# A fused layer (state-space scan plus experts) on one core: step 0's dt made in the first stage, x*D written straight into y's accumulator by ScalarE, softplus ahead of group 3's exponentials

## The chip, the core and the metric

The kernel runs on one core of a Trainium2 chip. The metric is the device time of one execution in microseconds (us), lower is better. The engines are named as in the profile: PE (TensorE: matmuls; PEld its weight loads), DVE (VectorE), ACT (ScalarE), POOL (GpSimd) and SP (SyncE, which here only issues DMAs). Each runs its own program in order, and they meet at semaphores. Everything is float32.

## What is computed

The input x has 2048 tokens of 512 features. The layer returns x + mamba(layernorm(x)) + experts(layernorm(x)):

```python
proj = hidden @ in_proj_w.T;  x, gate = split(proj)       # 1024 channels each
xt = silu(causal_conv4(x) + conv_b)
ts, B, C = split(xt @ x_proj_w.T)                         # 32, 16, 16 columns
dt = softplus(ts @ dt_proj_w.T + dt_proj_b)
state = state * exp(dt * A) + dt * B * x                  # per channel and 16 states, over time
y = (sum over states of state * C) + xt * D
out = (y * silu(gate)) @ out_proj_w.T
...
y = combine(silu(g) * u @ w_down)                         # 64 routed experts, top 6, 64 slots each
shared = silu(h @ sw_gate) * (h @ sw_up) @ sw_down
```

## The kernel before

There are three stages; a barrier of all engines stands between the first and the rest.

**Stage 1** (`stage1`) runs over four chunks of 512 tokens. It normalizes x, projects it (each matmul as three products of high and low parts; ACT makes the high part of a weight tile, `w_hi`, and POOL the low part, `w_lo`), convolves on DVE (`conv`), makes the router's scores and lists on DVE (`ranks`, `search`), and makes ts, B and C. SP stores what stage 2 needs and, in the last chunk, loads stage 2's first operands: the gate and up weights of the first expert pair, the tile of C (`load_C`), `load_dt` (ts and the weights of dt) and `load_xa` (xt). In the last chunk POOL also makes the first eight B diagonals.

**Stage 2** is 32 steps, one for 128 channels and 512 tokens; every step also does one pair of experts. Step i is written as i = 8c + d. A step has eight groups g of two states. In every group

- ACT copies the last column of a state buffer (`state_carry`) and makes two tiles `dA` = exp(dt * A) from `dt_blocks`, which holds dt spread over partitions;
- PE makes dt * B * x in PSUM (`dBx(i, cp, g)`, 64 short matmuls, tile p_dBx, two buffers). It first waits until the scan of group g-2 is done, which read the same buffer;
- DVE scans two states of 512 time steps (line 959), reading dA and p_dBx;
- POOL multiplies the states by C (line 894); PE adds these products over the states into the PSUM tile p_y (`sum_states(i, m, steps_ago)`, m = 0 for groups 0 to 3, m = 1 for groups 4 to 7; the latter runs in the next step, between dBx 2 and dBx 3).

The order on each engine is written out by hand. In PE's step it is dBx 0, `tokens_T`, `dt_proj(i+1)`, dBx 1, gate matmuls, dBx 2, sum_states of the last step's m = 1, `transpose_h`, dBx 3, half of the up matmuls, dBx 4, the other half, `dtx_T(i+1)`, dBx 5, `skip`, dBx 6, sum_states m = 0, dBx 7, `down`. `skip(i)` opens the accumulation of p_y: four identity matmuls that put x*D there, from a tile xD that ACT made at group 0 (`x_times_D`, line 1063) after waiting for the last step's m = 0 sum. DVE multiplies the finished p_y by the gate after the scan of group 3 (`gate`).

The dt of step i+1 is made within step i: `dt_proj`, softplus on ACT (`softplus_parts`, `softplus_log`: Abs, Relu, Exp, Ln, behind group 3's exponentials), `next_dt` and `next_dtx` on DVE behind the scan of group 1 (they make dt and dt*x in PSUM and SBUF), `take_dt` on ACT, then `spread_dt` on SP: 16 DMAs of 64 KB from SBUF to SBUF into `dt_blocks`, and `dtx_T`/`take_dtxT` for the transposed dt*x. For step 0 the same chain runs at the start of stage 2, before its first dBx. POOL meanwhile clears expert_y, expert_h, score_of_slot, silu's row and both buffers of the products, stores zeros in the spare rows of the experts' sums (DRAM tensor moe), and then gathers the first pair's tokens. ACT enters the loop after all buffers are cleared (s_c0) and those stores have landed (s_sc).

**Stage 3** computes the shared expert and the output projection and is not touched, but for the split of one buffer into two.

## Time and profile before

| | |
|---|---|
| median of 3 runs | 1401.55 us (1401.48 to 1403.74) |
| profiled execution, its own time | 1394.07 us |
| its span, first to last instruction | 1391.9 us |
| stage 1 ends, about | 267.7 us |
| stage 2 | 267.7 to 1089 us |
| busy: PE, DVE, ACT, POOL | 1307.6, 1093.6, 900.7, 882.9 us |
| mean granted TensorE clock | 0.983 |

Times in the rows are microseconds from the start of the span. A row of the timeline gives start, duration, engine, line, operation, output<-inputs, count, and in brackets the idle time before it and what ended it. Durations of neighbours overlap by some hundredths, so the step from one start to the next is the cost in a full queue.

### The profile page before, as it was taken

Reading aid. Unit: us, or ns where it says so; the run is one execution under the profiler, and the core shown is the slowest. Engines: PE = TensorE matmul, PEld = TensorE weight load, DVE = VectorE, ACT = ScalarE, POOL = GpSimd, SP = SyncE. Lnnn points to the kernel's source line nnn. Section 1 sums busy time; section 2 is a strip of 40 time slices with the busy share of each in tenths; the row PEclk is TensorE's granted clock in tenths of the full one; section 3 lists DMA queues with packets and bytes.
Section 4 is the critical chain, followed back from the end, with each engine's and each line's share of the span. In section 5 each row is a group of like instructions: output and inputs, shape, how many; then the busy total and the mean of one; then the engine's idle time right before and its main releaser. Section 6 shows DMA issues by size and latency. Waiting matters only on the chain.

```text
span 1391.9 us, 53931 instructions
## 1 busy us (share of the span) xinstructions
PE 1307.6 (94%) x21847; PEld 806.3 (58%) x21847; DVE 1093.6 (79%) x1259; ACT 900.7 (65%) x1912; POOL 882.9 (63%) x523
## 2 busy tenths in 40 slices
PE   4998989589999999999999999999999899999998
PEld 3767767345455545555545555445545577787876
DVE  4798989768988988889888898888888655655554
ACT  2756556378888778787887878867778343434343
POOL 2455357368898888988978889889898521303030
PEclk9999999789999999999999999999999999999999
DMA  7153535579899899898998989989889761313140
GB/s 287 65 223 117 197 131 204 176 195 307 264 290 286 248 289 278 274 302 238 307 268 256 298 260 292 294 248 293 271 250 298 251 230 50 132 37 144 35 146 31
DMA packets 129743, 304.84 MB, mean 219 GB/s; under 512 B 18512, under 2 KB 20304, under 8 KB 127888
## 3 DMA queue, kind: packets, MB, share of 16 engines
q1 hardware_dynamic: 122048, 285.13, 62.8%
q0 software_dynamic: 7632, 18.91, 6.0%
q8 instruction: 34, 0.56, 0.2%
q14 instruction: 29, 0.24, 0.1%
HBM read 213.65 MB, written 56.77 MB: 194 GB/s over the span
## 4 chain that ended last, share of the span: by engine, by line
PE 71%; DVE 4%; issue 3%; ACT 1%; DMA 1%; ACTq 0%; SPq 0%; DVEq 0%
PE p_dBx L1273 20%; PE p_y L1289 8%; PE p_dBx L1339 7%; PE p_g L1259 6%; PE p_u L1242 6%; PE p_g L1242 6%; PE p_dt L1222 3%; PE p_y L1350 2%; PE p_g L1350 2%; PE p_u L1350 2%; PE p_dt L1350 2%; PE p_y L1283 2%; PE p_u L1228 1%; DVE out_operand_parts L994 1%; PE p_dt L1235 1%
## 5 line engine op out<-in xcount | busy, mean ns | idle before, releaser
L959 DVE TENSOR_TENSOR_SCAN state<-dA,state_carry,p_dBx 128x512 f32<-128x512 f32 x512 | 626.7, 1266 | 87.2 <-PE p_dBx L1273 77.2
L894 POOL TENSOR_TENSOR h_times_C<-state,C_bcast 128x1024 f32<-128x1024 f32 x128 | 304.2, 2377 | 86.0 <-DVE state L959 85.2
L1106 ACT ACTIVATE dA<-dt_blocks,A_par 128x512 f32<-128x512 f32 x512 | 338.7, 709 | 18.9 <-DMA dt_blocks<-step_rows 18.8
L1273 PEld LDWEIGHTS p_dBx<-B_diagonals,step_rows 64*32 64x32 f32 x16384 | 236.1, 106 | 174.7 <-issue 174.6
L894 POOL TENSOR_TENSOR C_bcast<-state,C_bcast 128x1024 f32<-128x1024 f32 x128 | 320.0, 2787 | 17.6 <-DVE state L959 17.6
L1273 PE MATMUL p_dBx<-B_diagonals,step_rows 64*32 64x128 f32 x16384 | 314.0, 275 | 15.5 <-issue 14.5
L261 POOL TENSOR_TENSOR w_in_parts_lo<-C_bcast,w_in_parts_hi 128x512 fp32r<-128x512 f32 x64 | 89.8, 1405 | 123.1 <-ACT w_in_parts_hi L454 122.8
L909 POOL TENSOR_TENSOR step_rows<-step_rows 128x512 f32<-128x512 f32 x16 | 21.7, 1389 | 182.3 <-DMA step_rows<-moe 182.3
L1339 PE MATMUL p_dBx<-x_parts,shared_w_parts 128*128 128x512 f32 x528 | 127.3, 402 | 4.6 <-DVE shared_w_parts L988 4.6
L1339 PEld LDWEIGHTS p_dBx<-x_parts,shared_w_parts 128*128 128x128 f32 x528 | 100.6, 191 | 31.5 <-issue 7.4
L333 DVE SCALAR_TENSOR_TENSOR conv_out<-conv_in,conv_w,conv_out 128x512 f32<-128x512 f32 x96 | 94.7, 996 | 11.2 <-ACT conv_out L468 8.9
L1259 PE MATMUL p_g<-w_down_pair,step_rows 128*64 128x512 f32 (+1 forms) x396 | 92.3, 601 | 0.0
L1242 PE MATMUL p_u<-w_up_pair,step_rows 128*64 128x352 f32 x512 | 90.4, 472 | 1.3 <-issue 0.9
L454 ACT ACTIVATE w_in_parts_hi<-C_bcast 128x512 fp32r<-128x512 f32 x64 | 40.2, 630 | 73.6 <-PE p_in L577 65.9
L577 PE MATMUL p_in<-xT_parts_hi,w_in_parts_lo 128*128 128x512 f32 x256 | 72.9, 407 | 12.4 <-issue 6.1
L1242 PE MATMUL p_g<-w_gate_pair,step_rows 128*64 128x352 f32 x512 | 83.9, 470 | 0.3 <-ACT step_rows L1121 0.3
L1161 ACT ACTIVATE shared_h_rows<-p_dBx 128x512 f32<-128x512 f32 (+1 forms) x24 | 14.3, 597 | 104.9 <-PE p_dBx L1339 104.3
L874 POOL DMA_INDIRECT moe<-expert_y,scatter_rows x34 | 55.3, 1627 | 23.8 <-ACT expert_y L1079 18.6
L577 PE MATMUL p_in<-xT_parts_lo,w_in_parts_hi 128*128 128x512 f32 x256 | 69.5, 394 | 0.0
L577 PE MATMUL p_in<-xT_parts_hi,w_in_parts_hi 128*128 128x512 f32 x256 | 69.2, 392 | 0.0
L1010 DVE TENSOR_TENSOR shared_h_rows<-shared_h_rows,p_dBx 128x512 f32<-128x512 f32 (+1 forms) x24 | 16.5, 687 | 62.9 <-ACT shared_h_rows L1161 62.7
L1289 PE MATMUL p_y<-C_bcast,sum_over_states 128*32 128x512 f32 x528 | 63.5, 598 | 0.0
(172 smaller groups left out, 2018.4 us busy)
## 6 DMA issues: line engine op xcount, KB each, us to landing
w_gate_pair<-in_w_gate SPq DMA_DIRECT2D x32, 1408.0 KB
w_up_pair<-in_w_up SPq DMA_DIRECT2D x32, 1408.0 KB
w_down_pair<-in_w_down SPq DMA_DIRECT2D x66, 512.0 KB
dt_blocks<-step_rows SPq DMA_DIRECT2D x512, 64.0 KB
w_down_pair<-in_w_down SPq DMA_DIRECT2D x33, 384.0 KB
g_d<-y_gated SPq DMA_DIRECT2D x33, 256.0 KB, 4.8
sz_d<-silu_gate SPq DMA_DIRECT2D x32, 256.0 KB, 2.1
moe<-zeros SPq DMA_DIRECT2D x32, 256.0 KB, 3.0
```

What stands on the lines that cost most here:

```text
L261: pool.tensor_tensor(wp[1][:, n % 2, :], win[:, tile, :], wp[0][:, n % 2, :], ALU.subtract).then_inc(s_wlo, 1)
L333: ins = dve.scalar_tensor_tensor(xt[:, d, :], xr[:, d, k:k + CH], cw[:, d, k:k + 1], xt[:, d, :], ALU.mult, ALU.add)
L577: ins = pe.matmul(pIn[n % 2][:, :], wp[p][:, n % 2, k * P:(k + 1) * P], xp[q][:, c % 2, k, :], start=at == 0, stop=at == len(parts) - 1)
L894: pool.tensor_tensor(hc[m][:, b, :, :], hb[:, q, :, :], Cb[:, NM * cp + GS * m:NM * cp + GS * m + GS, :], ALU.mult).then_inc(s_hc, 1)
L959: ins = dve.tensor_tensor_scan(hb[:, g % NBUF, s, :], dA[:, g % NBUF, s, :], pB[:, g % 2, :].rearrange("p (t s) -> p s t", s=GS)[:, s, :], ...
L1106: ins = act.activation(dA[:, q, s, :], dtr[:, u, b, :], ACT.Exp, scale=A[:, bass.ds(d, 1), GS * g + s:GS * g + s + 1].rearrange("p a b -> ...
L1242: ins = pe.matmul(pX[r, 0:I], xgT[:, k, r], w[:, a, k, :], start=k == 0, stop=k == KH - 1)
L1259: ins = pe.matmul(pG[r, :], hT[0:k, m, r], wd[0:k, a, m, :], start=m == 0, stop=m == len(IK) - 1)
L1273: ins = pe.matmul(out[DB * p:DB * p + DB, half, j, :, :], dtxT[k, j * P + DB * b:j * P + DB * b + DB], diag[k, ND * cp + 2 * j + p // 2, a ...
L1289: ins = pe.matmul(pY[DB * b:DB * b + DB, :], sel4[:, :], hc[m][:, b, s, :], start=False, stop=m == 1 and s == GS - 1, skip_group_check=True)
L1339: ins = pe.matmul(pX[m % 2][:, :], wparts[:, m % 2, 2 * w + a, k, :], xp[x][:, k, :], start=at == 0, stop=at == len(parts) - 1)
L1350: ins = pe.matmul(pO[j][:, :], k_parts(p, k, 0)[:, j * P:(j + 1) * P], k_parts(q, k, 1), start=k == 0 and at == 0, stop=k == NK - 1 and at ...
```

## The change

1. **Step 0's dt in stage 1.** PE makes it at the end of the third chunk (into p_xT), ACT does Abs, Relu, Exp, Ln behind it (`first_softplus`), POOL the sum and dt*x in the fourth chunk behind its second `w_lo` (`first_dt`), SP the 16 spreading DMAs behind the load of the first gate weights. The tiles live in the unused end of the up weights' buffer; `dt_blocks` is split in an even and an odd tile, of which the even one doubles as stage 1's xn_T. Stage 2 starts with `dtx_T(0)`; its semaphores of step 0 are counted up.
2. **Start of stage 2.** POOL gathers first and clears three small buffers after it; the clears of the product buffers and of expert_y are gone. The zeros of moe's spare rows are copied from DRAM to DRAM at POOL's end of stage 1.
3. **x*D.** ACT writes it into p_y itself, at group 7 behind that group's exponentials; `skip` is gone, and PE waits for ACT ahead of the sum m = 0.
4. **Softplus** stands in front of group 3's carry copy and exponentials.

The core of the diff:

```diff
@@ SP, stage 1, last chunk
                     tile_in.load_gate(sp, 0)
+                    sp.wait_ge(s_dt0, 1)
+                    tile_in.load_dt(sp, 1)
+                    sp.wait_ge(s_xTs, 16 * NCH)
+                    sp.wait_ge(s_lps, NCH)
+                    sp.wait_ge(s_xlo, NCH)
+                    for b in range(NB):
+                        for p in range(NB):
+                            sp.dma_start(dtr0[DB * p:DB * p + DB, b, :], zl0[DB * b:DB * b + DB, :]).then_inc(s_spread, 16)
@@ POOL, stage 1
+            def first_dt():
+                pool.wait_ge(s_z0, 4)
+                pool.tensor_tensor(zl0, r0, zl0, ALU.add).then_inc(s_dt0, 1)
+                pool.wait_ge(tile_in.s_xa, 32)
+                pool.wait_ge(s_dt0, 1)
+                by_row = "p (i j r) -> p i j r"
+                pool.tensor_tensor(dtx[:, :].rearrange("p (j i r) -> p i j r", i=2, j=JD), zl0.rearrange(by_row, i=2, j=JD),
+                                   tile_in.xa[:, 0, :].rearrange(by_row, i=2, j=JD), ALU.mult).then_inc(s_dt0, 1)
...
+                    if c == NCH - 1 and n == 1:
+                        first_dt()
...
+            for a in range(2):
+                pool.dma_start(io["moe"][a * ROWS + T:(a + 1) * ROWS, :], io["moe"][a * ROWS:a * ROWS + CAP, :]).then_inc(keep["s_sc"], 16)
+                pool.wait_ge(keep["s_sc"], 16 * a + 16)
@@ ACT, stage 1
+            def first_softplus():
+                act.wait_ge(s_dt0ps, 1)
+                act.wait_ge(keep["s_par"], 48)
+                b = keep["dt_b"][:, 0:1]
+                act.activation(zl0, pT[:, 1, :], ACT.Abs, bias=b).then_inc(s_z0, 1)
+                act.activation(r0, pT[:, 1, :], ACT.Relu, bias=b).then_inc(s_z0, 1)
+                act.wait_ge(s_z0, 2)
+                act.activation(zl0, zl0, ACT.Exp, scale=-1.0).then_inc(s_z0, 1)
+                act.wait_ge(s_z0, 3)
+                act.activation(zl0, zl0, ACT.Ln, bias=1.0).then_inc(s_z0, 1)
@@ PE, stage 1, behind the x projection
+                if c == NCH - 2:
+                    pe.wait_ge(tile_in.s_wdt, 32)
+                    pe.wait_ge(s_xhi, NCH)
+                    pe.matmul(pT[:, 1, :], tile_in.wdt[:, :], tile_in.ts[:, :], start=True, stop=True).then_inc(s_dt0ps, 1)
@@ POOL, stage 2
-            pool.memset(yo[:, :, :], 0.0).then_inc(s_yz, 1)
-            for t in (hh[:, :], wsc[:, :], sz, hc[0], hc[1]):
-                pool.memset(t, 0.0).then_inc(s_c0, 1)
...
             gather(0, 0)
+            for t in (hh[:, :], wsc[:, :], sz):
+                pool.memset(t, 0.0).then_inc(s_c0, 1)
@@ ACT, stage 2
+            def x_times_D(i, u, d):
+                act.wait_ge(s_xa, 16 * i + 16)
+                act.wait_ge(s_g, i + 1)
+                act.activation(pY[:, :], xa[:, u, :], ACT.Copy, scale=d).then_inc(s_xD, 1)
...
-            act.wait_ge(s_sc, 32)
...
+                            if g == SOFTPLUS_AT:
+                                softplus_parts(i + 1, d + 1)
+                                softplus_log(i + 1)
                             act.wait_ge(s_scan, NG * i + (g + 1))
...
-                            if g == 0:
-                                act.wait_ge(s_sum, 2 * i + 1)
-                                act.wait_ge(s_xa, 16 * i + 16)
-                                x_times_D(u, Dp[:, bass.ds(d, 1)])
...
                             if g == NG - 1:
+                                x_times_D(i, u, Dp[:, bass.ds(d, 1)])
                                 take_dtxT(i + 1, 0, NG * i + 7)
@@ PE, stage 2
                     dBx(i, cp, 5)
-                    skip(i)
                     dBx(i, cp, 6)
+                    pe.wait_ge(s_xD, i + 1)
                     sum_states(i, 0, 0)
```

The end of a step on PE, before (line 1273 is dBx, 1283 the skip, 1289 sum_states, 1259 down):

```order
L1235 MATMUL p_dt<-identity,step_rows 128x128 x4
L1264 REGISTER_ALU
L1273 MATMUL p_dBx<-B_diagonals,step_rows 32x2x64 x32
L1283 MATMUL p_y<-step_rows,identity 32x512 x4
L1264 REGISTER_ALU
L1273 MATMUL p_dBx<-B_diagonals,step_rows 32x2x64 x32
L1289 MATMUL p_y<-h_times_C,sum_over_states 32x512 x8
```

and now (1313 is dBx, 1322 sum_states):

```order
L1275 MATMUL p_dt<-identity,dt_x 128x128 x4
L1304 REGISTER_ALU
L1313 MATMUL p_dBx<-B_diagonals,step_rows 32x2x64 x32
L1304 REGISTER_ALU
L1313 MATMUL p_dBx<-B_diagonals,step_rows 32x2x64 x32
L1322 MATMUL p_y<-h_times_C,sum_over_states 32x512 x8
```

Only the four matmuls between dBx 5 and dBx 6 are gone; everything else in the step keeps its place.

ACT between the third and the fourth chunk of stage 1, now (584 copies ts, B and C out; 529 to 534 are `first_softplus`; 541 and the rows behind it belong to the fourth chunk):

```order
L584 ACTIVATE x_proj_out<-p_logits_ssm 128x256
L529 ACTIVATE w_up_pair<-p_xT,dt_bias 128x512
L530 ACTIVATE w_up_pair<-p_xT,dt_bias 128x512
L532 ACT_TABLE_LOAD
L532 ACTIVATE w_up_pair<-w_up_pair 128x512
L534 ACT_TABLE_LOAD
L534 ACTIVATE w_up_pair<-w_up_pair 128x512
L541 ACTIVATE conv_in<-conv_in 128x8x3
L485 ACTIVATE w_in_parts_hi<-C_bcast 128x512
L498 ACTIVATE conv_in<-p_in 128x512
```

Before, the copy out and the fourth chunk's first row stood next to each other; four activations and two table loads are new between them, and a third load stands in front of the fourth chunk's first Silu.

POOL at the start of stage 2, before (844 to 847 clear and set, 850 stores the zeros, 854 and 860 gather step 0's tokens):

```order
L844 MEMSET expert_y 128x1024
L846 MEMSET expert_h 128x352
L846 MEMSET score_of_slot 128x34
L846 MEMSET step_rows 128x512
L846 MEMSET h_times_C 128x4096
L846 MEMSET C_bcast 128x4096
L847 IOTA scatter_rows 128x2
L850 DMA moe<-expert_y 64x512 x2
L854 COPY gather_rows<-gather_lists 128x1
L860 DMA tokens_of_pair<-xn_d,gather_rows 128x576
```

and now:

```order
L894 COPY gather_rows<-gather_lists 128x1
L900 DMA tokens_of_pair<-xn_d,gather_rows 128x576
L920 MEMSET expert_h 128x352
L920 MEMSET score_of_slot 128x34
L920 MEMSET step_rows 128x512
L921 IOTA scatter_rows 128x2
```

The gather moved from behind everything to the front; three of the clears and the stores are gone from here.

## Rows read from the trace of the kernel before

**Rows 1.** Windows: stage 1's last stretch, and the steps of stage 2.
```profile
196.00:267.00 71.00, 59.68 (x322) 43.43 (x320) 68.18 (x109) 33.63 (x60) 34.25 (x25) 0.96 0.58 208
361.70:1089.00 727.30, 711.95 (x17651) 367.72 (x17649) 638.84 (x611) 573.98 (x1323) 631.18 (x348) 1.00 0.91 277
```
In these rows stand: from:to, length, busy us (and count) of PE, PEld, DVE, ACT, POOL, granted clock, DMA share, GB/s.

**Rows 2.** Timeline of PE, one step of stage 2.
```profile
386.64 1.16 PE L1273 MATMUL p_dBx<-B_diagonals,step_rows 64*32 64x128 f32 x64
...
394.37 0.70 PE L1273 MATMUL p_dBx<-B_diagonals,step_rows 64*32 64x128 f32 x24 [0.38 <-issue]
...
397.33 1.16 PE L1273 MATMUL p_dBx<-B_diagonals,step_rows 64*32 64x128 f32 x64
...
403.85 1.06 PE L1283 MATMUL p_y<-step_rows,identity 128*32 128x512 f32 x8
404.85 1.16 PE L1273 MATMUL p_dBx<-B_diagonals,step_rows 64*32 64x128 f32 x64
...
411.60 0.66 PE L1273 MATMUL p_dBx<-B_diagonals,step_rows 64*32 64x128 f32 x31
```

**Rows 3.** Timeline of DVE, the same step.
```profile
387.96 2.45 DVE L959 TENSOR_TENSOR_SCAN state<-dA,state_carry,p_dBx 128x512 f32<-128x512 f32 x2 [0.78 <-PE p_dBx L1273]
...
393.79 0.70 DVE L926 TENSOR_TENSOR p_dt<-p_dt,step_rows 128x512 f32<-128x512 f32 x1 [0.56 <-ACT step_rows L1051]
...
395.22 2.45 DVE L959 TENSOR_TENSOR_SCAN state<-dA,state_carry,p_dBx 128x512 f32<-128x512 f32 x2
398.65 2.45 DVE L959 TENSOR_TENSOR_SCAN state<-dA,state_carry,p_dBx 128x512 f32<-128x512 f32 x2 [0.98 <-PE p_dBx L1273]
401.02 0.67 DVE L941 TENSOR_TENSOR y_gated<-p_y,step_rows 128x512 f32<-128x512 f32 x1
401.61 4.95 DVE L959 TENSOR_TENSOR_SCAN state<-dA,state_carry,p_dBx 128x512 f32<-128x512 f32 x4
```

**Rows 4.** Timeline of ACT, the same step.
```profile
402.07 1.32 ACT L1106 ACTIVATE dA<-dt_blocks,A_par 128x512 f32<-128x512 f32 x2
...
408.19 0.72 ACT L1063 ACTIVATE step_rows<-xt_for_dtx,D_par 128x512 f32<-128x512 f32 x1 [1.65 <-PE p_y L1289]
```

**Rows 5.** Timeline of all engines, start of stage 2.
```profile
269.31 0.48 DVE L920 MEMSET p_g<- 128x512 f32 x1
...
275.81 10.16 SPq L759 DMA_DIRECT2D dt_blocks<-step_rows  x16
...
275.93 1.09 PE L1235 MATMUL p_dt<-identity,step_rows 128*128 128x128 f32 x4 [5.21 <-ACT step_rows L1059]
...
277.68 1.96 PE L1273 MATMUL p_dBx<-B_diagonals,step_rows 64*32 64x128 f32 x64 [0.67 <-ACT step_rows L1071]
...
278.95 1.06 POOL L860 DMA_INDIRECT tokens_of_pair<-xn_d,gather_rows  x1 [0.89 <-POOL gather_rows L854]
...
280.50 0.20 ACT L1101 ACTIVATE state_carry<-state 128x2 f32 x1 [3.06 <-DMA moe<-expert_y]
...
283.73 1.13 PE L1228 MATMUL p_u<-identity,tokens_of_pair 128*128 128x128 f32 x4 [4.09 <-DMA tokens_of_pair<-xn_d,gather_rows]
...
285.99 2.06 PE L1222 MATMUL p_dt<-ts_tile,w_dt 32*128 32x512 f32 x2 [1.12 <-ACT step_rows L1071]
...
289.87 3.72 PE L1242 MATMUL p_g<-w_gate_pair,step_rows 128*64 128x352 f32 x16
```

**Rows 6.** Stage 1, last chunk: timelines of ACT, SP, POOL, and a DVE group.
```profile
222.41 1.28 ACT L473 ACT_TABLE_LOAD   x1
...
246.77 0.32 SPq L187 DMA_DIRECT2D sz_d<-silu_gate  x1
...
206.77 1.27 POOL L261 TENSOR_TENSOR w_in_parts_lo<-C_bcast,w_in_parts_hi 128x512 fp32r<-128x512 f32 x1 [6.50 <-ACT w_in_parts_hi L454]
...
L333 DVE SCALAR_TENSOR_TENSOR conv_out<-conv_in,conv_w,conv_out 128x512 f32<-128x512 f32 x4 | 2.9, 751 | 0.1
...
L333 DVE SCALAR_TENSOR_TENSOR conv_out<-conv_in,conv_w,conv_out 128x512 f32<-128x512 f32 x9 | 10.9, 1215 | 0.2
```
The last two are groups by line (busy us, mean ns, idle before): of 186 to 196 us, with POOL mostly idle or in one long operation, and of 213 to 236 us, with POOL in its short ones.

More of the change, by code:

```diff
@@ L78, in stage1 @@
         xp = [sb(f"xT_parts_{n}", [P, 2, KH, CH], F32R) for n in ("hi", "lo")]
[L79 removed]
+        dtr0, dtx = keep["dtr0"], keep["dtx"]
+        xnT = dtr0
         wgate = sb("w_router", [P, KH, E])
@@ L98, in stage1 @@
         ixf = sb("top8_index_f", [P, TJ, 8])
-        eioi = sb("expert_iota_i", [P, TJ, E], I32)
+        with ExitStack() as own:
+            eioi = own.enter_context(nc.sbuf_tensor("expert_iota_i", [P, TJ, E], I32))
+        chosen = sb("chosen", [P, TJ, E])
         eio = sb("expert_iota", [P, TJ, E])
@@ L105, in stage1 @@
         eq = tile_in.wu[:, :, :, :].rearrange("p a k i -> p (a k i)")[:, 0:TOPK * TJ * E].rearrange("p (k n) -> p k n", k=TOPK)
-        chosen = sb("chosen", [P, TJ, E])
+        wu_flat = tile_in.wu[:, :, :, :].rearrange("p a k i -> p (a k i)")
+        zl0, r0 = (wu_flat[:, TOPK * TJ * E + n * CH:TOPK * TJ * E + (n + 1) * CH] for n in range(2))
         val = sb("rank_if_chosen", [P, TJ, E])
@@ L659, in stages2and3 @@
         rows2 = sb("step_rows", [P, 2 * TJ, CH])
-        zl, dts, dtx, dtxT, sz, xD = (rows2[:, n, :] for n in range(6))
+        zl, dts, dtxT, sz = (rows2[:, n, :] for n in range(4))
         xgT = rows2[:, 6, :].rearrange("p (k s) -> p k s", k=KH)
@@ L843, in _ @@
         def _(pool):
-            pool.memset(yo[:, :, :], 0.0).then_inc(s_yz, 1)
-            for t in (hh[:, :], wsc[:, :], sz, hc[0], hc[1]):
-                pool.memset(t, 0.0).then_inc(s_c0, 1)
-            pool.iota(si[:, :], [[0, 2]], base=T, channel_multiplier=1).then_inc(s_si, 1)
-            pool.wait_ge(s_yz, 1)
-            for a in range(2):
-                pool.dma_start(io["moe"][a * ROWS + T:(a + 1) * ROWS, :], yo[0:CAP, 0, :]).then_inc(s_sc, 16)
             def gather_rows(n, u):
@@ L941, in gate @@
                 dve.tensor_tensor(gb[:, u, :], pY[:, :], sz, ALU.mult).then_inc(s_g, 1)
-            next_dt(0)
-            next_dtx(0, 0)
+            for s_first in (s_dt, s_dtx):
+                dve.sem_inc(s_first, 1)
             dve.wait_ge(s_c0, CLEARED)
@@ L1059, in take_dt @@
                 act.activation(dts, pM[:, :], ACT.Copy).then_inc(s_dtc, 1)
-            def x_times_D(u, d):
-                act.activation(xD, xa[:, u, :], ACT.Copy, scale=d).then_inc(s_xD, 1)
+            def x_times_D(i, u, d):
+                act.wait_ge(s_xa, 16 * i + 16)
+                act.wait_ge(s_g, i + 1)
+                act.activation(pY[:, :], xa[:, u, :], ACT.Copy, scale=d).then_inc(s_xD, 1)
             def take_dtxT(n, part, used):
@@ L1276, in dBx @@
                 ins.then_inc(s_bps, 1)
-            def skip(i):
-                pe.wait_ge(s_g, i + 1)
-                pe.wait_ge(s_xD, i + 1)
-                for b in range(NB):
-                    own = slice(DB * b, DB * b + DB)
-                    pe.matmul(pY[own, :], ident[:, own], xD, start=True, stop=False, skip_group_check=True)
             def sum_states(i, m, steps_ago):
@@ L1291, in sum_states @@
                 ins.then_inc(s_sum, 1)
-            dt_proj(0)
+            pe.sem_inc(s_dtps, 1)
             dtx_T(0)
```

50 lines of the change are left out of this document (28 added, 22 removed).

## The prediction

> **What bounds the kernel now.** I read the windows by stage first, then the timeline of one step of stage 2 engine by engine, then the start of stage 2, and last the end of stage 1. In the windows [rows 1] PE is busy for 711.95 of 727.30 us of the steps (98%), DVE 88%, POOL 87%, ACT 79%, the DMA engines 91%, at the full granted clock of 2.4 GHz. So PE sets the pace of stage 2. The timeline of PE [rows 2] says the same: one step runs from the first dBx at 386.64 to the next at 411.60, 24.96 us, and the rows stand back to back. The one exception is a pause inside dBx 2, whose second part starts at 394.37 with "issue" as its releaser, 7.73 us behind the step's start. It is no wait for an engine, and the change puts nothing in front of it; I leave it as it is. DVE waits for PE: 0.78 us before the scan of group 0 and 0.98 us before that of group 3 [rows 3].
>
> Ahead of the steps lies a chain in which little overlaps. After the barrier at about 267.7, step 0's dt is made, and the first dBx starts at 277.68 only [rows 5]. It runs at half the clock: 1.96 us, against 1.16 in the steps [rows 2]. The chain then has two more waits: ACT enters its loop at 280.50, after 3.06 us for the zeros stored to moe, and PE gets step 0's tokens at 283.73, because POOL issued their gather at 278.95 only, behind its clears.
>
> The end of stage 1 is DVE's: busy 68.18 of 71.00 us [rows 1], while PE, ACT and POOL have room. What is put on those three there is paid only if it reaches DVE.
>
> **The skip in the step.** Removed: four matmuls, from 403.85 to the start of dBx 6 at 404.85, 1.00 us of PE's queue [rows 2]. Not all of it can be had. dBx 6 overwrites the PSUM buffer that the scan of group 4 reads, so it cannot start before that scan is done. From dBx 3 on, DVE is a chain of its own [rows 3]: the scan of group 3 starts at 398.65, as soon as dBx 3 (397.33) is done, then comes the gate at 401.02, then four scans at 401.61 taking 4.95, of which the first two are group 4: done at 401.61 + 2.47 = 404.08. With about 0.15 us for the hand-over (dBx 3 ends at 397.33 + 1.16 = 398.49 and its scan starts at 398.65), dBx 6 starts at 404.23, not at 403.85. The gain is 404.85 - 404.23 = 0.62 us a step, and 0.38 becomes a new wait of PE for DVE.
>
> Does the 0.62 survive to the step's end? Everything on PE behind dBx 6 shifts as a block, and the next dBx 0 starts at 411.60 - 0.62 = 410.98. The scan of the next group 0 then waits for PE 0.78 - 0.62 = 0.16 us instead of 0.78 [rows 3], so DVE is just not the bound there. The next dBx 3 stands at the same distance from dBx 0 as now, so the period is 24.96 - 0.62 = 24.34. Over 32 steps: -0.62 x 32 = **-19.8 us**. The DMA engines, at 91% of 24.96 = 22.7 us, still fit into 24.34.
>
> **x*D on ACT.** It now stands behind group 7's exponentials at 402.07 [rows 4]. These end at 403.39; with 0.1 for the hand-over and 0.72 for the row at 408.19, x*D is in p_y at 404.2. PE wants it behind dBx 6, at 404.23 + 1.08 = 405.3. So the new wait of PE for ACT is covered with 1.1 us to spare. What ACT itself waits for, the gate's end on DVE at 401.02 + 0.67 = 401.7, is past. I take 0.72 for a write to PSUM, since the trace has no such row of Copy with scale from SBUF; it could take 1.1 longer before it cost anything. What is queued behind it on ACT is the copy of dt*x transposed, which PE needs only at the next dBx 0, 6 us later. At group 0 the old place disappears with its 1.65 us of waiting for PE; ACT is not the bound, so this is worth nothing.
>
> **Softplus earlier.** DVE waits 0.56 us for it at 393.79. But the scan behind it, at 395.22, waits for dBx 2 anyway, whose last matmuls end at 394.37 + 0.70 = 395.07 [rows 2, 3]. So the 0.56 turns into a wait for PE: 0 us. The exponentials of group 3 become 2.7 us later, and their scan comes at 398.65, over 4 us behind them: no cost either.
>
> **Start of stage 2.** What is left before the first dBx: DVE's last clear, 269.31 + 0.48 = 269.8; `dtx_T(0)` at 269.9 in place of 275.93; the first dBx 1.75 us behind it as before (277.68 - 275.93), at 271.7. POOL gathers at once: its descriptor row stood 1.1 us behind the copy ahead of it, so 268.8, and tokens arrive 283.73 - 278.95 = 4.78 us later, at 273.6, just when the first dBx ends. ACT starts its exponentials at 272 without the 3.06. Two groups at 1.32 + 0.20 each (the rows at 402.07 and 280.50) and the second half of the transposed dt*x, about 0.4, take it to 275.4; `dt_proj(1)` then starts at 275.4 in place of 285.99, and with the same distance as before (289.87 - 285.99 = 3.88) the gate matmuls start at 279.3 in place of 289.87: **-10.6 us**. At the granted clock, half until 292 in this profile, there may be more: PE would now work without long gaps from 271.7, and if the clock rises up to 3 us sooner than the shift alone gives, up to 1.5 us come on top. I take 0.9, giving **-11.5**. The spreading DMAs, 10.16 us at 275.81 [rows 5], are off this path. The up weights of step 0 keep their place as last load of stage 1.
>
> **Stage 1.** ACT gets four activations of 0.6 to 0.7 us (like x*D's row) and three table loads of 1.28 [rows 6], PE one projection (about 1 us at full clock), POOL two operations of about 1.3 each by its `w_lo` at 206.77. That `w_lo` follows 6.50 us of idling, so this is where POOL takes them; the third weight tile becomes low-part-ready near 213.5, and PE's third projection about 1.5 us later than now. DVE is at that time busy with searches and the first convolution, so nothing of this is on its path. But POOL's catching up is: a DVE convolution takes 751 ns with POOL quiet and 1215 with POOL in its short operations [rows 6]. About 3.5 us of POOL's work moves from under the searches to under the convolutions; beside it DVE loses (1215 - 751)/1215 = 38% of its pace, which costs 3.5 x 0.38 = **+1.3 us** (0 if POOL has slack enough, 3 if its own two operations also fall there). SP issues the 16 spreads in 10.2 us from 237.4 on, and its next store is due at 246.77 [rows 6]: late by 0.8, covered since C and the stores are waited for only at the barrier.
>
> By the table load's row the three cost 3.84 us, and the activation follows without a gap. The Trainium skill (ScalarE: Activation LUTs, What ACT_TABLE_LOAD costs) adds a drain of about 1.4 us to each switch; by that rule ACT would be 4.1 us later, POOL would move some 3 us more work under the convolutions, and the sum would be about 1 us higher. The trace of before does not show the drain where the load stands in a running queue.
>
> **The sum.** -19.8 - 11.5 + 1.3 = -30.0 us. Against the profiled execution, 1394.07 becomes 1364.1 (span 1361.9). The median of the runs shown stands 7.5 us above that execution; I take the difference as it is: 1401.55 - 30.0 = **1371.5 us**.
>
> **The rivals.**
> - *The step keeps less.* Each hand-over that becomes tight (scan to dBx 6, dBx 0 to scan) costs some tenths more, because a stopped PE queue has to be refilled; "issue" rows of 0.38 us exist [rows 2]. At 0.3 us less a step: 9.6 us, 1381. For it: DVE's slack at group 0 shrinks to 0.16, POOL and the DMA engines are near 90% too. Against: the rows left add up without it.
> - *The loop gains nothing, only the start does.* Then x*D or the scans take exactly the time that the skip took: -11.5 + 1.3 gives 1391. For it: DVE's chain from 398.65 is unbroken to the next group 0. Against: its 0.78 us there.
> - *More than forecast.* The pause in dBx 2 shrinks too or the first steps run at full clock: up to 0.3 us a step, 1362.
> - *Slower.* ACT is an in-order queue, and PE now stands still for it every step. If x*D lands later than 405.3, each us costs 32. It outweighs both gains once it comes 0.62 + (11.5 - 1.3)/32 = 0.94 us a step behind that, that is 2.0 us later than I compute; at 2.5 us later the time is 1401.55 + 0.5 x 32 = 1418. For it: the diagonals (eight activations) stand just ahead of group 7. Against: they were in the row's start of 402.07 already.
>
> **How the numbers follow.** My forecast 0.54 (its own range 1366 to 1376), less in the step 0.17, only the start 0.11, more 0.12, slower 0.04, and 0.02 for gains that cancel. A measurement tells 0.2% (2.8 us) from no change. The range reaches from the "more" case to between the two cases of lower gain: 1361 to 1386, leaving out the case of the start alone and the slow one, and a small part of "more". Faster 0.94, same 0.02, slower 0.04.
>
> **What would show it.** The distance of two first dBx in stage 2: 24.3 (24.96 if the loop gains nothing). An idle stretch of about 0.4 us before dBx 6, released by DVE's scan, and no idle time of PE before the sum behind it. The gate matmuls of step 0 start near 279 to 281, 11.6 us behind the barrier (22.2 before). The DVE row of next_dt no longer waits for ACT, and its scan still waits for PE. The barrier at 268 to 270. I am wrong if the period does not move, if PE waits for ACT's x*D, or if stage 1 ends more than 3 us later.

## The result and the profile after

The changed kernel takes 1390.36 us (median of 4, 1388.11 to 1390.8), the kernel before beside it 1401.51: ratio 0.9923, 95% interval 0.9905 to 0.9941. It is faster, by 11 us (0.8%, clear of the noise), not by the 30 forecast. The profiled execution takes 1388.11 us (span 1386.3) against 1394.07, only 6.0 less; the rest of the difference of the medians lies in executions of before that were slower than its profiled one.

The windows of the changed kernel, same stages as [rows 1]:

```profile
196.00:267.00 71.00, 61.11 (x322) 43.75 (x321) 68.95 (x100) 40.13 (x67) 38.45 (x29) 0.97 0.59 198
355.80:1083.00 727.20, 697.97 (x17399) 368.32 (x17399) 637.59 (x610) 580.74 (x1324) 630.77 (x348) 1.00 0.91 277
```

The steps hold as much work of DVE and POOL per us as before, while PE is busy 14 us less: PE does less in the same time. The timeline of PE, one step, against [rows 2]:

```profile
582.17 1.16 PE L1313 MATMUL p_dBx<-B_diagonals,step_rows 64*32 64x128 f32 x64
...
588.59 0.97 PE L1313 MATMUL p_dBx<-B_diagonals,step_rows 64*32 64x128 f32 x44
589.90 0.66 PE L1313 MATMUL p_dBx<-B_diagonals,step_rows 64*32 64x128 f32 x20 [0.33 <-issue]
...
592.82 1.16 PE L1313 MATMUL p_dBx<-B_diagonals,step_rows 64*32 64x128 f32 x64
...
599.68 1.15 PE L1313 MATMUL p_dBx<-B_diagonals,step_rows 64*32 64x128 f32 x64 [0.27 <-DVE state L1002]
600.76 1.92 PE L1322 MATMUL p_y<-h_times_C,sum_over_states 128*32 128x512 f32 x16
602.61 1.56 PE L1313 MATMUL p_dBx<-B_diagonals,step_rows 64*32 64x128 f32 x64
...
606.83 1.16 PE L1313 MATMUL p_dBx<-B_diagonals,step_rows 64*32 64x128 f32 x64
```

dBx 3 to dBx 6 takes 599.68 - 592.82 = 6.86 us, 0.66 less than the 7.52 of [rows 2], and dBx 6 waits for the scan: the forecast's mechanism, and its 0.62 to within 0.04 us. But dBx 7 now takes 1.56 us instead of 1.16, and the step is 606.83 - 582.17 = 24.66 here; the ones around it alternate between this and 25.14. Inside dBx 7 is a pause near its 34th matmul, for which the trace names no releaser.

ACT and DVE in the same step, against [rows 3, 4]:

```profile
597.56 1.32 ACT L1152 ACTIVATE dA<-dt_blocks_even,A_par 128x512 f32<-128x512 f32 x2
598.79 0.67 ACT L1108 ACTIVATE p_y<-xt_for_dtx,D_par 128x512 f32<-128x512 f32 x1
```
```profile
588.68 0.67 DVE L969 TENSOR_TENSOR p_dt<-p_dt,step_rows 128x512 f32<-128x512 f32 x1
589.46 0.69 DVE L976 TENSOR_TENSOR dt_x<-p_dt,xt_for_dtx 128x512 f32<-128x512 f32 x1
590.70 2.45 DVE L1002 TENSOR_TENSOR_SCAN state<-dA,state_carry,p_dBx 128x512 f32<-128x512 f32 x2 [0.56 <-ACT dA L1152]
```

x*D is done at 599.46, 1.3 us before the sum wants it, and costs 0.67 us into PSUM. DVE's `next_dt` no longer waits, and its 0.56 us stands in front of the scan of group 2 instead. That scan also needs dBx 2, whose last matmuls end at 589.90 + 0.66 = 590.56, so the label ACT is only the later of two near equals.

Start of stage 2, all engines, against [rows 5]:

```profile
267.66 0.40 SPq L1438 DMA_DIRECT2D w_up_pair<-in_w_up  x1
270.57 1.58 SPq L801 DMA_DIRECT2D w_down_pair<-in_w_down  x3
```
```profile
271.28 1.08 POOL L900 DMA_INDIRECT tokens_of_pair<-xn_d,gather_rows  x1 [0.90 <-POOL gather_rows L894]
271.30 1.09 PE L1275 MATMUL p_dt<-identity,dt_x 128*128 128x128 f32 x4 [2.27 <-DVEq L987]
...
273.82 1.96 PE L1313 MATMUL p_dBx<-B_diagonals,step_rows 64*32 64x128 f32 x64 [1.43 <-POOL step_rows L920]
...
279.32 1.13 PE L1268 MATMUL p_u<-identity,tokens_of_pair 128*128 128x128 f32 x4 [3.54 <-DMA tokens_of_pair<-xn_d,gather_rows]
280.38 2.07 PE L1262 MATMUL p_dt<-ts_tile,w_dt 32*128 32x512 f32 x2
...
284.85 3.58 PE L1282 MATMUL p_g<-w_gate_pair,step_rows 128*64 128x352 f32 x16
```

The gather takes 279.32 - 271.28 = 8.04 us instead of 4.78, while 1.4 MB of up weights and then the down weights are on their way. The gate matmuls start at 284.85 instead of 289.87: 5.0 us earlier, where the forecast's 10.6 less stage 1's 1.3 gave 9.3. The clock came with them and not sooner: the granted clock is 0.50 up to 286 us and 1.00 from 288 on, and in the trace of before 0.50 up to 292 and 1.00 from 294 on.

Stage 1, where ACT's table loads and POOL's added work stand (against [rows 6]):

```profile
205.39 1.28 ACT L532 ACT_TABLE_LOAD   x1
206.69 0.63 ACT L532 ACTIVATE w_up_pair<-w_up_pair 128x512 f32<-128x512 f32 x1
207.33 1.28 ACT L534 ACT_TABLE_LOAD   x1
208.63 0.63 ACT L534 ACTIVATE w_up_pair<-w_up_pair 128x512 f32<-128x512 f32 x1
```
```profile
209.34 1.29 POOL L293 TENSOR_TENSOR w_up_pair<-w_up_pair 128x512 f32<-128x512 f32 x1 [9.03 <-ACT w_up_pair L534]
...
214.26 1.91 POOL L276 TENSOR_TENSOR w_in_parts_lo<-C_bcast,w_in_parts_hi 128x512 fp32r<-128x512 f32 x1
```
```profile
214.28 3.90 DVE L364 SCALAR_TENSOR_TENSOR conv_out<-conv_in,conv_w,conv_out 128x512 f32<-128x512 f32 x3
```

DVE's first convolution of the chunk takes 3.90 us for three operations (2.31 in the trace of before) because POOL catches up beside it. DVE's searches end level in the two traces (their last maximum starts at 213.00, before 212.96); by the router's scores DVE is 1.9 us behind (228.22 against 226.29). POOL's first instruction behind the barrier, the gather's copy, starts at 270.20, against 267.74: 2.4 us later than before.

### The profile page after: what moved, and what is told of

Its sections match the earlier page's. It is cut to its first block, busy times and chain, and to the rows that moved or that the text cites. A ratio compares the mean times of both kernels' runs of the same rounds, so it can differ in the third digit from the quotient of the medians.

```text
span 1386.3 us, 53429 instructions
## 1 busy us (share of the span) xinstructions
PE 1291.9 (93%) x21591; PEld 808.3 (58%) x21591; DVE 1095.9 (79%) x1257; ACT 910.5 (66%) x1914; POOL 878.1 (63%) x522
## 4 chain that ended last, share of the span: by engine, by line
PE 61%; DVE 11%; issue 6%; DVEq 1%; DMA 1%; ACT 0%; POOL 0%; ACTq 0%; POOLq 0%
PE p_dBx L1313 18%; PE p_y L1322 9%; DVE state L1002 8%; PE p_dBx L1372 7%; PE p_g L1299 6%; PE p_g L1282 6%; PE p_dt L1262 2%; PE p_y L1383 2%; PE p_g L1383 2%; PE p_u L1383 2%; PE p_dt L1383 2%; PE p_u L1268 2%; DVE out_operand_parts L1037 2%; PE p_u L1289 1%; PE p_u L1282 1%
## 5 line engine op out<-in xcount | busy, mean ns | idle before, releaser
L1313 PE MATMUL p_dBx<-B_diagonals,step_rows 64*32 64x128 f32 x16384 | 327.9, 275 | 30.0 <-issue 20.4
L1313 PEld LDWEIGHTS p_dBx<-B_diagonals,step_rows 64*32 64x32 f32 x16384 | 242.3, 106 | 178.8 <-issue 176.8
L1152 ACT ACTIVATE dA<-dt_blocks_odd,A_par 128x512 f32<-128x512 f32 x256 | 169.7, 710 | 14.8 <-DMA dt_blocks_odd<-step_rows 14.8
L1152 ACT ACTIVATE dA<-dt_blocks_even,A_par 128x512 f32<-128x512 f32 x256 | 169.7, 710 | 4.2 <-DMA dt_blocks_even<-step_rows 4.2
L364 DVE SCALAR_TENSOR_TENSOR conv_out<-conv_in,conv_w,conv_out 128x512 f32<-128x512 f32 x96 | 100.4, 1055 | 10.3 <-ACT conv_out L499 8.0
L1201 ACT ACTIVATE shared_h_rows<-p_dBx 128x512 f32<-128x512 f32 (+1 forms) x24 | 14.3, 596 | 103.4 <-PE p_dBx L1372 102.9
L1372 PE MATMUL p_dBx<-x_parts,shared_w_parts_even 128*128 128x512 f32 x288 | 70.3, 401 | 4.7 <-DVE shared_w_parts_even L1031 4.7
L1147 ACT ACTIVATE state_carry<-state 128x2 f32 x256 | 49.7, 194 | 30.1 <-DVE state L1002 24.9
L1372 PEld LDWEIGHTS p_dBx<-x_parts,shared_w_parts_even 128*128 128x128 f32 x288 | 55.3, 194 | 19.3 <-issue 7.4
```

Source lines behind the costliest of these rows:

```text
L364: ins = dve.scalar_tensor_tensor(xt[:, d, :], xr[:, d, k:k + CH], cw[:, d, k:k + 1], xt[:, d, :], ALU.mult, ALU.add)
L1152: ins = act.activation(dA[:, q, s, :], dtr[u][:, b, :], ACT.Exp, scale=A[:, bass.ds(d, 1), GS * g + s:GS * g + s + 1].rearrange("p a b -> ...
L1313: ins = pe.matmul(out[DB * p:DB * p + DB, half, j, :, :], dtxT[k, j * P + DB * b:j * P + DB * b + DB], diag[k, ND * cp + 2 * j + p // 2, a ...
L1372: ins = pe.matmul(pX[m % 2][:, :], wparts[m % 2][:, 2 * w + a, k, :], xp[x][:, k, :], start=at == 0, stop=at == len(parts) - 1)
```

## The experiments

They ran on several chips, which fall into two groups, and this matters. In group A (the result and the first four runs) the kernel before takes 1399.3 to 1401.5 us, in group B (all others, three chips) 1380.6 to 1383.5. I compare within a group. Mean distances on PE, worked out from its timeline over steps 3 to 30 without the first step of each chunk (25 steps), in us:

| kernel | dBx 0 to sum m = 1 | dBx 3 to dBx 6 | dBx 6 to next dBx 0 | step |
|---|---|---|---|---|
| A: before | 8.33 | 7.52 | 6.80 | 24.98 |
| A: changed | 8.46 | 6.86 | 7.31 | 24.96 |
| A: xd_only | 8.43 | 6.86 | 7.30 | 24.92 |
| A: skip_back | 8.33 | 7.51 | 6.79 | 24.96 |
| A: softplus_back | 8.43 | 6.86 | 7.29 | 24.91 |
| A: pad32 | 8.32 | 11.28 | 8.74 | 30.66 |
| B: before_again | 7.56 | 7.57 | 6.76 | 24.22 |
| B: after_again | 7.87 | 6.88 | 6.85 | 23.93 |
| B: xd_only_again | 7.82 | 6.88 | 6.84 | 23.87 |
| B: after_no_weights | 7.92 | 6.87 | 6.82 | 23.94 |
| B: half_dBx7 (median) | 7.51 | 6.86 | 6.26 | 22.97 |

**xd_only, xd_only_again.** Before, with the x*D edit of ACT and PE only; PE's part of it:

```diff
-                    skip(i)
                     dBx(i, cp, 6)
+                    pe.wait_ge(s_xD, i + 1)
                     sum_states(i, 0, 0)
```

> The kernel before with one edit: ACT writes x*D into p_y, the skip's four matmuls are gone. Softplus and the start of stage 2 are as before. Three theories. (1) Instruction order bound: PE's instructions meet a pause at fixed places of the step's program; the skip's time goes into a second pause inside dBx 7. Then the step stays 24.9 to 25.05 us, the time within 3 us of before, dBx 3 to dBx 6 is 6.86 us instead of 7.52, and inside dBx 7 there is a pause of 0.3 to 0.5 us near its 34th matmul. (2) DVE's chain bounds the step: the same time, but no pause inside dBx 7; PE's idle time stands in front of dBx 6 and dBx 0, released by DVE. (3) The loop gain of the forecast exists and the softplus order takes it away: step 24.3 to 24.7, time 9 to 20 us under before.

Measured in A: 1394.13 us, ratio 0.9964 (0.9949 to 0.9978); 3 to 6 is 6.86, and the time comes back in dBx 7. This is theory 1's picture, not 2's, though the median is 5.2 us lower, more than its 3: the steps give 0.06 each, 1.9 in all, and where the other 3 us lie is open.

> The kernel before with the x*D edit alone, as in the first call, on this core. If the skip's removal alone brings the pauses: on a core where the kernel before has none, a median step of 23.9 to 24.0 with a pause at the end of dBx 2, 0.25 to 0.3 us shorter than before, and 7 to 11 us less in all (ratio 0.992 to 0.995); the rest of the changed kernel's gain of 14.4 us there, 4 to 6 us, is then the start's. If the start or the earlier softplus brings them: no pause, a step of 23.6 us, 19 us less.

In B: 1370.64, ratio 0.9905 (0.9873 to 0.9937), step 23.87, with a pause of 0.1 to 0.4 us at the end of dBx 2 that before_again has not. So removing the skip brings the pause by itself. The 12.9 us in the medians are more than the 7 to 11 expected. They leave 1.5 us to the start, where 4 to 6 were expected; the two intervals, 0.9873 to 0.9937 here and 0.9861 to 0.9912 for the whole change, overlap too far to tell.

**skip_back.** The changed kernel with the skip again, and x*D at its old place at group 0.

> The changed kernel with the skip's four matmuls and xD's old place at group 0 put back; the new start and the earlier softplus stay. If the gain of the change is all at the start of stage 2 and in the first three steps, the time is that of the changed kernel within 3 us (1388 to 1393) and a median step is 24.9 to 25.0 us. If the removed skip is worth something in the loop that the two profiles did not show, the time is 5 us or more above the changed kernel.

1393.14, ratio 0.9961 (0.9946 to 0.9977), no pause in dBx 7. The start's part (with softplus) is thus 6.2 us in the medians. It stands at the bound of what was expected, and the two parts add up: 5.2 + 6.2 = 11.4, against 11.15 for the whole change.

**softplus_back.** The block of `SOFTPLUS_AT` behind the exponentials again.

> The changed kernel with softplus behind group 3's exponentials again. The changed kernel's steps alternate between 24.66 and 25.14 us. If the late exponentials of group 3 cause the long ones (DVE's scan of group 3 late, PE's dBx 5 late), all steps come to 24.66 and the time is about 7 us lower, 1381 to 1384. If the pauses on PE cause them, the alternation stays and the time is within 2.5 us of the changed kernel.

1391.74 (0.9931 to 0.997); steps still alternate between 24.6 and 25.1. Moving softplus is worth nothing that shows, and does not cause the alternation.

**pad32.** Changed, with

```diff
+                    for _ in range(32):
+                        pe.sem_inc(s_past, 1)
                     dBx(i, cp, 6)
```

> The changed kernel with 32 semaphore increments more in PE's program of each step, in front of the wait of dBx 6, where PE stands still for DVE anyway. Nothing is computed otherwise. (1a) PE's instructions are supplied at a limited rate, about 27 matmuls with their weight loads per us: 32 instructions more cost 0.4 to 0.6 us a step, 13 to 19 us. (1b) The pauses sit at fixed places of the program: the pause inside dBx 7 comes 16 matmuls earlier (about the 18th of dBx 7 instead of the 34th), and the time moves under 5 us. (2) If the pause hangs on an event of another engine, it stays at the same time and the same matmul, and the time does not move.

1567.06, ratio 1.1201: none of the theories. Timeline of PE:

```profile
733.99 1.16 PE L1313 MATMUL p_dBx<-B_diagonals,step_rows 64*32 64x128 f32 x64
739.85 1.96 PE L1313 MATMUL p_dBx<-B_diagonals,step_rows 64*32 64x128 f32 x64 [4.69 <-issue]
741.74 3.17 PE L1322 MATMUL p_y<-h_times_C,sum_over_states 128*32 128x512 f32 x16
```

32 increments hold PE 4.69 us, 0.15 each. dBx 6 then takes 1.96 us, as in [rows 5], and the granted clock is 0.50 there (739.85 to 741.74). Almost nothing was hidden: dBx 3 to dBx 6 grows by 11.28 - 6.86 = 4.42 us. So hardly any matmul can have been queued ahead of PE at the end of dBx 5. The pause in dBx 7 is gone; that in dBx 2 is as before.

**dtxT_later, sum_first, half_dBx4, up_split.** Changed, each with one edit:

```diff
# dtxT_later
-                    dtx_T(i + 1)
                     dBx(i, cp, 5)
+                    dtx_T(i + 1)
# sum_first
-                    dBx(i, cp, 2)
                     sum_states(i, 1, 1)
+                    dBx(i, cp, 2)
# half_dBx4 (half_dBx7: g == 7)
-                for j in range(JD):
+                for j in range(JD // 2 if g == 4 else JD):
# up_split
+                            for h in range(2):
+                                cols = slice(I // 2 * h, I // 2 * h + I // 2)
```

> The changed kernel with dtx_T(i+1), four transposes of 0.66 us together, moved from in front of dBx 5 to behind it, so that it fills PE's new wait in front of dBx 6 (0.27 us idle, 0.53 from start to start). Supply theory (PE's instructions come at a limited rate, and the program is at that limit): the wait of dBx 6 goes, the pause in dBx 7 grows by the same, the median step stays 24.85 to 25.05 us, the time within 3 us of the changed kernel. DVE theory (the hand-overs between scan and dBx set the step, the pauses are of a fixed length): a step is 0.2 to 0.3 us shorter, 6 to 10 us in all.

> The changed kernel with the sum m = 1 in front of dBx 2 instead of behind it: 16 matmuls that take 1.9 us, so that PE reaches the 192nd matmul of the step 1.3 us later. Supply theory: the pause of 0.6 us that stands at the 42nd matmul of dBx 2, 7.7 us behind the step's start, disappears or shrinks to under 0.2 us, but pauses elsewhere (dBx 3 to dBx 7) grow by as much: the step stays 24.8 to 25.05 us. Event theory (the pause hangs on that place of the program or on a time): a pause of 0.6 us stays in dBx 2. Independent pauses: it vanishes and nothing takes its place, step 24.3 to 24.5, 15 to 20 us less in all.

> The changed kernel with 32 of the 64 matmuls of dBx 4 left out (the products of group 4's second half of channels stay what they were). DVE's chain from dBx 3 to dBx 6 is untouched, so dBx 3 to dBx 6 stays 6.86 us and PE's wait there grows from 0.5 to 1.0 us. Supply theory: 32 matmuls fewer before dBx 7, and no pause is left in dBx 7, step 24.3 to 24.6 us, 10 to 19 us less in all. Place theory (the pause belongs to a fixed place of the program, whatever came before): a pause of 0.3 to 0.5 us stays 560 matmuls behind the step's start or in dBx 7, step 24.85 to 25.0.

> The changed kernel with each up matmul (352 columns) made as two of 176: 16 matmuls more in a step, the same columns. Supply theory: the pause in dBx 7 grows by 16/26.5 = 0.6 us, median step 25.4 to 25.6 us, 15 to 20 us more in all. If only PE's columns and DVE's chain count: under 0.15 us a step, under 5 us in all.

These were the first in group B (before: 1381.79), and their expectations are in group A's figures. Medians 1367.14, 1378.19, 1361.39, 1366.91; mean steps 23.99, 24.29, 23.91, 23.93, against after_again's 23.93 on another chip of the group. On these cores dBx 7 has hardly a pause to begin with, so the four runs do not decide between the theories of the pause there. dtxT_later, half_dBx4 and up_split show that more or fewer matmuls between dBx 3 and the wait of dBx 6 change nothing: DVE's chain sets that stretch at 6.86 to 6.9, and the pause in dBx 2 stays. sum_first removes the pause of dBx 2, but that scan starts later and the wait moves in front of dBx 6 (7.64 for 3 to 6): worse.

**before_again, after_again.** Both kernels unchanged, in B.

> The kernel before once more, for a trace on the same core as the changed kernel. The last four kernels ran where the kernel before takes 1381.8 us at the median instead of 1401.5 or 1399.3, and there the pause in dBx 2 is 0.2 us long instead of 0.6. If the pauses belong to the core and not to the program, the time of the kernel before goes with them: where its dBx 2 pause is 0.6 us, its median step is 24.93 and its time 1394 to 1404; where it is 0.2 us, the step is 24.3 to 24.5 and the time 1378 to 1386.

> The changed kernel once more, for the same reason. If the pauses set what the skip is worth: on a core with the 0.6 us pause, a median step of 24.85 to 25.05, no shorter than before, a pause of 0.3 to 0.5 us in dBx 7, and a time ratio of 0.992 to 0.996; on a core with the 0.2 us pause, no pause in dBx 7, a step 0.3 to 0.6 us shorter than before, and a ratio of 0.982 to 0.990. If the pauses have no part in it (DVE's chain or the start decide), the ratio and the gain per step are the same on both.

1384.57 (one run) and 1366.14 us, the latter with ratio 0.9887 (0.9861 to 0.9912). PE, before_again and then after_again, from dBx 0 on:

```profile
587.17 1.16 PE L1273 MATMUL p_dBx<-B_diagonals,step_rows 64*32 64x128 f32 x64
...
593.59 1.18 PE L1273 MATMUL p_dBx<-B_diagonals,step_rows 64*32 64x128 f32 x64
594.71 1.92 PE L1289 MATMUL p_y<-C_bcast,sum_over_states 128*32 128x512 f32 x16
```
```profile
570.84 1.16 PE L1313 MATMUL p_dBx<-B_diagonals,step_rows 64*32 64x128 f32 x64
...
577.26 1.59 PE L1313 MATMUL p_dBx<-B_diagonals,step_rows 64*32 64x128 f32 x64
578.77 1.92 PE L1322 MATMUL p_y<-C_bcast,sum_over_states 128*32 128x512 f32 x16
...
587.97 1.16 PE L1313 MATMUL p_dBx<-B_diagonals,step_rows 64*32 64x128 f32 x64 [0.28 <-DVE state L1002]
```

Here before has no pause at all (593.59 - 587.17 and 1.18 are back to back), and the changed kernel gets one: dBx 2 takes 1.59. The step gains 0.69 in front of dBx 6 and loses 0.31 in dBx 2 and 0.09 behind dBx 6: 0.29 in all, 9 us over the loop, just under the 0.3 expected. The kernel before has no 0.2 us pause here, as I had supposed, but none.

**before_no_up, after_no_up, after_no_weights.** Weight loads of steps 1 and later replaced by increments, for instance

```diff
-                    tile_in.load_up(sp, i + 1)
+                    sp.sem_inc(s_wu, 16)
```

> The kernel before with the loads of the up weights of steps 1 and later left out (1.4 MB of some 6.8 MB a step; the same weights are used again). Two theories of PE's pauses inside dBx. DMA theory: PE's program comes late because the DMA engines are 91 to 95% busy; with a fifth less traffic the pauses shrink to under 0.1 us, the step is 24.2 us or less on any core. Own-limit theory: the pauses come from PE's instruction supply alone, whatever the DMA engines do: where the kernel before has a 0.6 us pause it stays, step 24.9; where it has none, step 24.2.

> The changed kernel with the same loads left out. DMA theory: the pauses in dBx 2 (0.2 or 0.6 us) and in dBx 7 go, and the step comes to the forecast's arithmetic, 24.20 - 0.62 = 23.6 us, every step alike. Own-limit theory: the step stays at 23.9 (or at 24.9 where the pauses are long), with the pauses where they are.

> The changed kernel with the loads of gate, up and down weights of steps 1 and later all left out; the DMA engines then have about a third of their traffic. DMA theory: as with the up loads left out or better, 23.5 to 23.65 us a step. Own-limit theory: the same step as the changed kernel, 23.9 or 24.9, pauses unmoved. If one third of the way shows in the first run and the rest here, the pauses go with the traffic.

Steps 24.23, 23.94, 23.94; single runs of 1372.92, 1357.63 and 1352.28 us. Windows of after_again, then of after_no_weights:

```profile
361.00:1030.00 669.00, 652.31 (x16522) 345.79 (x16518) 604.69 (x579) 548.00 (x1270) 598.15 (x329) 1.00 0.94 285
```
```profile
361.00:1000.00 639.00, 631.70 (x16068) 335.44 (x16068) 589.33 (x564) 539.97 (x1242) 582.88 (x323) 1.00 0.45 109
```

With the DMA share down from 0.94 to 0.45 the step and its pauses are the same. The DMA theory of the pauses falls, for group B; in group A it was not tested.

**half_dBx7.** 32 of dBx 7's matmuls left out.

> The changed kernel with 32 of the 64 matmuls of dBx 7 left out (0.55 us of PE; group 7's products of half the channels stay what they were). The traffic of the DMA engines did not move the pause at the end of dBx 2 (0.4 us behind what back-to-back work gives), and matmuls left out in front of dBx 6's wait did not either. What is left is the stretch from that wait to the pause: 367 matmuls in 14.4 us. Supply theory (PE's queue of instructions catches up while PE waits and runs out after so many matmuls in so short a time): with 32 fewer in 13.8 us the pause in dBx 2 goes: dBx 0 to the sum behind dBx 2 takes 7.53 us instead of 7.95, the step is 23.93 - 0.55 - 0.4 = 23.0 us, or what DVE's chain then sets, 23.0 to 23.3. Place theory (the pause belongs to this place or time behind the loop's branch): it stays, 7.9 us, and the step is 23.93 - 0.55 = 23.4 us.

PE:

```profile
563.51 1.16 PE L1313 MATMUL p_dBx<-B_diagonals,step_rows 64*32 64x128 f32 x64
...
569.93 1.16 PE L1313 MATMUL p_dBx<-B_diagonals,step_rows 64*32 64x128 f32 x64
571.02 1.92 PE L1322 MATMUL p_y<-C_bcast,sum_over_states 128*32 128x512 f32 x16
...
586.47 1.16 PE L1313 MATMUL p_dBx<-B_diagonals,step_rows 64*32 64x128 f32 x64
```

The pause in dBx 2 is gone (7.51 from dBx 0 to the sum), and the step is 586.47 - 563.51 = 22.96: the supply theory's 23.0, not 23.4. The median step is 22.97; the mean is 23.23, because 7 of the 25 steps are 0.2 to 3.3 us longer. Time 1343.2 us in one run.

**up_late, up_late_dtxT, up_late_clears.** Changed, with

```diff
+            sp.wait_ge(s_xg, 16)
+            tile_in.load_up(sp, 0)
             load_wd(0)
```

instead of `load_up(0)` at the end of stage 1, so that the up and the down weights both come behind the gather; the second also has dtxT_later's edit, the third the clears ahead of the gather.

> The changed kernel with step 0's up weights (1.4 MB) and down weights loaded only once step 0's tokens have landed, instead of from the end of stage 1 on. Contention theory: the gather took 8.04 us in the changed kernel because it shares the DMA engines with these loads (4.78 us before); it then lands in 4.5 to 5.5 us, PE's tokens_T of step 0 starts near 276 to 277 instead of 279.3 (with the barrier at 270.1), and the time falls by 1.5 to 3 us, less what the up matmuls now wait for their weights. If POOL's own descriptor work sets the gather's time, it stays near 8 us and the time does not fall.

> Both: the late loads of step 0's up and down weights, and dtx_T(i+1) behind dBx 5, where it fills PE's wait for the scan. If both are worth something, 3 to 10 us less than the changed kernel: dBx 6 without its wait of 0.5 us. On a core with pauses of 0.6 us the supply theory gives nothing for the second part (a step of 24.85 to 25.05), on one with 0.2 us up to 0.2 us a step.

> The changed kernel with step 0's up and down weights loaded once the tokens have landed, and POOL's three small clears in front of the gather instead of behind it. PE's first dBx waited 1.4 to 1.5 us for the clears, which stood behind the gather's descriptors. Now they end about 1.1 us sooner and the gather is issued 0.9 us later: the first dBx near 272.9 instead of 273.9, the tokens near 276.7 instead of 275.85. If the tokens bound the start, it is 0 to 1 us slower than with the late loads alone; if the first dBx does, up to 1 us faster. Against the changed kernel 4 to 6 us faster either way.

PE in up_late:

```profile
273.95 1.96 PE L1314 MATMUL p_dBx<-B_diagonals,step_rows 64*32 64x128 f32 x64 [1.52 <-POOL step_rows L921]
275.85 1.13 PE L1269 MATMUL p_u<-identity,tokens_of_pair 128*128 128x128 f32 x4
276.97 2.06 PE L1263 MATMUL p_dt<-ts_tile,w_dt 32*128 32x512 f32 x2
...
280.85 3.27 PE L1283 MATMUL p_g<-w_gate_pair,step_rows 128*64 128x352 f32 x16
```

The tokens are there when dBx 0 ends (275.85). The gather, issued at 271.38, had landed by 275.00, when SP issues the load that waits for it: 3.6 us. The gate matmuls start at 280.85, 3.6 us before after_again's 284.47. Time 1360.30 us, ratio 0.9854 (0.9825 to 0.9882), 5.8 us under after_again in the medians, where 1.5 to 3 were expected; the intervals overlap, the trace carries the finding. It is the best complete version that I ran. The other two, 1362.48 (0.9843 to 0.9893) and 1364.02 (0.9837 to 0.9895), are no better in their times, and the last misses the 4 to 6 us expected. With the clears first, though, the stretch from POOL's first copy to the gate matmuls is 282.00 - 272.19 = 9.81 us against 280.85 - 270.28 = 10.57 in up_late: 0.8 us, too little for the medians.

## Why the prediction was wrong

**Of its steps, in group A's profile.** The forecast -30.0 was -5.6 of span. From step 1's dBx 0 to the end, before takes 1391.90 - 311.24 and the changed kernel 1386.26 - 306.15: -0.6 instead of -19.2 (31 steps). Up to that point: -5.1 instead of some -10.8. The median missed by 18.9 (1390.36 against 1371.5).

**"Everything on PE behind dBx 6 shifts as a block"** is the step that failed, with "I leave it as it is" for the pause in dBx 2. The gain at dBx 6 came as computed (0.66 for 0.62; 0.69 in B), the wait there too, and x*D was early enough. But PE does not take up the new distance: it paused elsewhere, for 0.51 us behind dBx 6 and 0.13 in dBx 2 in A, for 0.4 in B. So the next dBx 0 was hardly earlier, and DVE's wait in front of group 0's scan fell in the mean of the same 25 steps only from 0.82 to 0.69 us in A and from 0.77 to 0.32 in B, not to 0.16. xd_only and xd_only_again show that the skip's removal alone brings this.

I had read "issue" as a fixed thing. It is not: in B it appears only when the skip is gone. From the start of the skip to the 211th matmul of the next step, before_again issues 375 matmuls in 15.0 us (24.9 per us) without a pause; after_again, from dBx 6's start, 367 in 14.3 (25.7) with one; half_dBx7 335 in 13.7 (24.4) and in 23 of 25 steps without. So it is not the number alone, for the most matmuls had no pause; that it is their density in this stretch fits the three and is argued, not shown. Shown is that 32 matmuls fewer take B's pause away, and that neither the DMA traffic (after_no_weights) nor the earlier softplus (xd_only_again has it in its old place) makes it. What limits the issue is open. So is why A's pause in dBx 2 sits within a few matmuls of the 192nd, about 0.6 us long, in the kernel before, the changed one, skip_back and pad32 alike, though in pad32 the stretch ahead of it is 1.9 us longer than before. Whether A's pause in dBx 7 has B's cause was not tested there: its going in pad32 fits, no more.

**The rivals.** "The loop gains nothing, only the start does" gave 1391 and had 0.11. Its number came true in A, by luck: neither x*D nor the scans took the time, and by the medians 5.2 us came with the skip's removal and 6.2 with the start, not 10.2 with the start alone. "The step keeps less" is the nearest: B's loss is 0.62 - 0.29 = 0.33 a step where it said 0.3. Its reason, a queue that refills at each tight hand-over, no run shows; the pauses stand elsewhere. I gave that 0.17; the trace of before held a sign, an "issue" pause in a full step of a 98% busy PE.

**Start of stage 2.** Mis-sized. The 4.78 us of the gather are from a place where the DMA engines moved 196 GB/s; moved forward, it meets the up and down weights, at 316 GB/s, and takes 8.04 (6.7 to 8.7 in all twelve traces with this start and these loads). up_late shows it: 3.6 without them, at 81 GB/s. I had moved the gather and left the loads beside it. From POOL's first instruction behind the barrier to the gate matmuls it is 22.1 us before and 14.7 now, where I had 11.6; up_late has 10.57. That is 3.1 of the 5.7 missing up to step 1; stage 1 has 1.1. Behind the gate matmuls only 0.1 more came, not the 0.9 that I added for the clock, which no trace shows, and step 0's 0.62. The first dBx, at 273.82, came 3.6 us behind the barrier, where I had 4.0, but not by my reason: `dtx_T(0)` came sooner (1.1 us behind it, not 2.2), and the clears stood behind the gather's descriptors on POOL, a queue that I had not walked (1.43 us of waiting).

**Stage 1.** +2.4 us between these two traces instead of +1.3: POOL's catching up under the convolutions was right in kind and too small (1.9 us from 213 to 228 us). But one pair of traces is thin here. POOL's first instruction behind the barrier stands between 267.7 and 272.4 us, mean 270.3, in the five traces with before's stage 1, and between 270.1 and 274.6, mean 272.1, in the twelve with the changed one: +1.8. Part of that spread is the clock: from 60 to 260 us the granted clock is 1.00 in the trace of before and 0.97 in before_again and xd_only, whose stage 1 is the same and ends 4.6 and 3.3 us later. The Trainium skill's drain of about 1.4 us at each table switch (ScalarE: Activation LUTs, What ACT_TABLE_LOAD costs) does not show here: the activations follow their loads by 1.30 us from start to start, and ACT runs on.

**The median.** I carried the 7.5 us between before's profiled run and its median over; the changed kernel's is 2.3. That is 5 us of luck in my favour: against the profiled runs the forecast missed by 24.

## What to carry to other kernels

An idle stretch with "issue" as its releaser, in a queue that is otherwise full, can be a resource at its limit: time taken out of PE elsewhere can come back there, so price a PE saving by the waits it meets, and give a chance of its own to the short matmuls behind it issuing no faster than now. Look at the same pause on more than one core before building on it. And when a transfer is moved earlier, list what is in flight at its new place: here putting the weight loads behind the gather brought the gate matmuls 3.6 us forward, and the median 5.8 us down, in intervals that overlap, on top of the whole change's 14.4 on those cores.
